# A fused expert-attention-expert block: the last expert queue of phase 2 added on VectorE, values' remainders earlier in attention's first stage, and fewer fillers ahead of it

## The reference

```
x = x + 0.5 * ffn(layernorm(x))       # phase 1: experts "e1"
x = x + attention(layernorm(x))       # 4 heads of 32, delta rule in chunks of 32
x = x + 0.5 * ffn(layernorm(x))       # phase 2: experts "e2"
```

## Time and profile before

| | |
|---|---|
| median of three runs | 917.46 us |
| lowest and highest of them | 914.82 and 926.24 us |
| the profiled execution | 921.84 us, its span 920.0 us |
| PE busy | 845.3 us (92%) |
| DVE busy | 547.2 us (59%) |
| POOL busy | 500.8 us (54%) |
| ACT busy | 392.8 us (43%) |
| mean granted clock of TensorE | 0.953 of full speed |

### The profile page before, as it was taken

The page is one execution under the profiler, slowest core; times in us unless marked ns, Lnnn a source line. Parts: engine busy times, 40 slices in busy tenths (PEclk is TensorE's granted clock), DMA queues, the critical chain, the costliest instruction groups (busy, mean ns, idle before and its releaser), DMA issues. The chain is left out here.

```text
span 920.0 us, 26251 instructions
## 1 busy us (share of the span) xinstructions
PE 845.3 (92%) x10885; PEld 747.1 (81%) x10885; DVE 547.2 (59%) x1645; ACT 392.8 (43%) x850; POOL 500.8 (54%) x631
## 2 busy tenths in 40 slices
PE   8479999999979789999999899998989999999996
PEld 7358999999967566788778776877767899999996
DVE  4745665555557945658485936484573556656662
ACT  4634444444314432266346542562542544444431
POOL 2658889866630721582228623882445444346667
PEclk8569999999989899899999999999998999999998
DMA  9454677444222110012001121111112644445544
GB/s 310 111 117 122 214 232 251 133 137 135 61 85 58 24 33 18 4 24 54 20 5 30 38 75 39 22 35 52 51 47 78 223 154 153 128 128 115 118 67 36
DMA packets 75475, 85.97 MB, mean 93 GB/s; under 512 B 9767, under 2 KB 62163, under 8 KB 74332
## 3 DMA queue, kind: packets, MB, share of 16 engines
q1 hardware_dynamic: 61148, 63.74, 23.3%
q0 software_dynamic: 14208, 20.55, 9.7%
HBM read 46.70 MB, written 34.01 MB: 88 GB/s over the span
## 5 line engine op out<-in xcount | busy, mean ns | idle before, releaser
L1020 DVE TENSOR_TENSOR e_hid<-e_sg,e_pu 128x320 f32<-128x320 f32 x256 | 124.7, 488 | 160.5 <-ACT e_sg L961 153.9
L961 ACT ACTIVATE e_sg<-e_pg 128x320 f32<-128x320 f32 x256 | 111.9, 438 | 208.5 <-PE e_pg L918 208.1
L282 POOL DMA_INDIRECT queue<-wide_rows,slot x64 | 64.9, 1014 | 89.5 <-ACT wide_rows L568 21.1
L1112 POOL TENSOR_TENSOR first_rows<-a_inv,a_nmat 128x135 f32<-128x135 f32 (+20 forms) x116 | 61.2, 527 | 68.7 <-DVE a_nmat L1965 60.2
L916 PE MATMUL e_pg<-e_xlo,e_whi 128*128 128x320 f32 x256 | 96.6, 377 | 0.9 <-DVE e_xlo L983 0.5
L904 PE MATMUL e_po<-e_expert,e_hid 128*128 128x128 f32 x640 | 83.7, 275 | 1.3 <-DVE e_hid L1020 1.3
L904 PE MATMUL e_po<-expert,e_hid 128*128 128x128 f32 x640 | 84.2, 274 | 0.0
L904 PEld LDWEIGHTS e_po<-e_expert,e_hid 128*128 128x128 f32 x640 | 79.9, 191 | 1.8 <-DVE e_hid L1020 1.8
L904 PEld LDWEIGHTS e_po<-expert,e_hid 128*128 128x128 f32 x640 | 80.3, 191 | 0.1
L917 PE MATMUL e_pg<-e_xhi,e_wlo 128*128 128x320 f32 x256 | 79.7, 311 | 0.0
L918 PE MATMUL e_pu<-e_xhi,e_whi 128*128 128x320 f32 x256 | 79.5, 310 | 0.0
(11 more groups left out here) (379 smaller groups left out, 2076.8 us busy)
## 6 DMA issues: line engine op xcount, KB each, us to landing
expert<-wexp_in SPq DMA_DIRECT2D x14, 512.0 KB, 4.4
e_expert<-wexp_in SPq DMA_DIRECT2D x14, 512.0 KB, 4.4
line<-blank SPq DMA_DIRECT2D x3, 1310.0 KB, 7.4
e_xs<-queue SPq DMA_DIRECT2D x12, 327.5 KB, 4.9
e_xs<-line SPq DMA_DIRECT2D x6, 647.5 KB, 6.4
expert<-wexp_in SPq DMA_DIRECT2D x14, 256.0 KB, 2.8
e_expert<-wexp_in SPq DMA_DIRECT2D x14, 256.0 KB, 3.5
queue<-blank SPq DMA_DIRECT2D x2, 1310.0 KB, 9.3
```

The source lines that it names most:

```text
L282: pool.indirect_dma_start(io.queue, bass.IndirectOffsetOnAxis(ap=k.slot[:, j, 1:2], axis=0), k.xn[:, j, :], None, bounds_check=SLOTS - 1, ...
L961: act.activation(sg[n % 2][:], pg[n % 2][:, 0:HALF], ACT.Silu).then_inc(silued, 1)
L1020: dve.tensor_tensor(hid[q % 2][:, f, c * HALF:c * HALF + HALF], sg[n % 2][:], pu[n % 2][:, 0:HALF], ALU.mult).then_inc(hidden, 1)
L1112: link(eng.tensor_tensor(part, bc(inv[:, j:j + 1, own], shape), bc(factor, shape), ALU.mult))
```

## The change

Four edits.

1. **Phase 2's last queue.** Its token numbers and weights are loaded on their own (`ahead`, one transfer on SP's queue in its iteration q = 6) and `index` for it runs in q = 7 on VectorE. After the first eight queues' transfers have landed, POOL gathers the rows of `out` that belong to the last queue's tokens into `rest` (five indirect transfers) and waits for them, then goes on with the tiles of queues 8 to 15. VectorE adds `rest` while it writes out the last queue's products, and POOL sends these with `replace` in place of `add_up`.
2. **The order of the three terms of the scales, in all stages:** the product with `vlo` comes last of three. Of the first half of a group, the first matmul waits for `vhi`, and only the third for `vlo`.
3. **VectorE in attention's first stage:** the second half of `vlo` after step 7 in place of step 10; `low_rows(1)` after step 25, ahead of the last six steps and of `prepare`, in place of after `prepare`. `SPLIT` is 6 in place of 8: VectorE inverts 6 columns, POOL 26.
4. **Fillers:** 40 in place of 56 ahead of attention's first transposes; 10 new ones in the first stage ahead of the scales.

```
+        rest = None if raw else sb("rest", [P, CT, D])
+        ahead = None if raw else sb("ahead", [P, CT, ROW - D])
...
+                if not raw and q + 2 == E:
+                    sp.dma_start(ahead[:], io.queue[SLOTS - CAP:SLOTS, D:ROW].rearrange(
+                        "(s p) d -> p s d", p=P)).then_inc(peeked, 16)
...
-                if half and q // E in BY_TOKEN:
-                    index(q)
+                if half and q // E in BY_TOKEN and (raw or q < LAST):
+                    index(q, rows_of(q)[:, :, D:ROW])
...
+                    if not raw and q == LAST:
+                        dve.wait_ge(foretold, 1)
+                        dve.wait_ge(restored, 16 * CT)
+                    elif not raw:
                         dve.wait_ge(indexed, numbered(q))
...
-                elif q < E:
+                elif q < E or q == LAST:
                     dve.scalar_tensor_tensor(rows[q % NR][:, s, :], down_bank(tile), factor[:, q, s:s + 1],
-                                             rows_of(q)[:, s, ROW:WIDE], ALU.mult, ALU.add).then_inc(rready, 1)
+                                             rows_of(q)[:, s, ROW:WIDE] if q < E else rest[:, s, :],
+                                             ALU.mult, ALU.add).then_inc(rready, 1)
...
+                    if not raw and q + 1 == E and n == REST_AT:
+                        dve.wait_ge(peeked, 16)
+                        index(LAST, ahead[:])
...
-                    put = deliver if raw else replace if q < E else add_up
+                    put = deliver if raw else replace if q < E or q == LAST else add_up
...
                 keep_tiles(0, CT * E)
                 all_stored(pool, 0)
+                pool.wait_ge(foretold, 1)
+                for s in range(CT):
+                    gather(pool, io.out, token[:, LAST, s:s + 1], rest[:, s, :], restored)
+                pool.wait_ge(restored, 16 * CT)
                 keep_tiles(CT * E, CT * NQ)
...
-        SPLIT = 8
+        SPLIT = 6
+        ROWS_IN = 25
...
                     elif first:
-                        pe.wait_ge(silued, UNITS * a + 6 - bank)
+                        pe.wait_ge(vhigh, 2 * a + 2)
+                    if i == TERMS - 1 and not half:
                         pe.wait_ge(vlow, 2 * a + 2)
...
-                        x, w = ((vhi, k.lag_hi), (vlo, k.lag_hi), (vhi, k.lag_lo))[term]
+                        x, w = ((vhi, k.lag_hi), (vhi, k.lag_lo), (vlo, k.lag_hi))[term]
...
+                if not here:
+                    keep_clock(pe, k, pp[:, 0, :], 10)
                 part = filler(6)
...
-            keep_clock(pe, k, pp[:, 0, :], 56)
+            keep_clock(pe, k, pp[:, 0, :], 40)
             turn(0, (0,))
...
                     low_values(a, 0)
-                    invert_first(5, 10)
+                    invert_first(5, 7)
                     low_values(a, 1)
+                    invert_first(7, 10)
                     cross_values(a)
-                    invert_first(10, CHUNK - 1)
+                    invert_first(10, ROWS_IN)
+                    low_rows(g + 2, 0)
+                    low_rows(g + 2, 1)
+                    invert_first(ROWS_IN, CHUNK - 1)
...
                 if ahead:
                     prepare(a)
-                if later:
+                if later and here:
                     low_rows(g + 2, 0)
-                if later:
                     low_rows(g + 2, 1)
```

More of the change, by code:

```diff
@@ L751, in experts @@
         downed, rready, indexed = sem("downed"), sem("rready"), sem("indexed")
+        peeked, foretold, restored = (None if raw else sem(n) for n in ("peeked", "foretold", "restored"))
         stored = [[sem(f"stored{i}") for i in range(NR)], k.delivered] if raw else k.stored
@@ L989, in evacuate @@
                     rows_free(dve, q)
-                    if not raw:
+                    if not raw and q == LAST:
+                        dve.wait_ge(foretold, 1)
+                        dve.wait_ge(restored, 16 * CT)
+                    elif not raw:
                         dve.wait_ge(indexed, numbered(q))
@@ L1000, in evacuate, with index @@
                                       ALU.mult).then_inc(rready, 1)
-            def index(q):
-                row = rows_of(q)
+            def index(q, row):
                 if raw:
-                    dve.tensor_scalar(token[:, q, :], row[:, :, D], float(APART), None, ALU.add).then_inc(indexed, 1)
+                    dve.tensor_scalar(token[:, q, :], row[:, :, 0], float(APART), None, ALU.add).then_inc(indexed, 1)
                 else:
-                    dve.tensor_copy(factor[:, q, :], row[:, :, D + 1 + q // E])
+                    dve.tensor_copy(factor[:, q, :], row[:, :, 1 + q // E])
                     spare = C_TRASH + q % 2 * CT
-                    dve.scalar_tensor_tensor(token[:, q, :], row[:, :, D], float(2 * APART),
-                                             k.const[:, spare:spare + CT], ALU.add, ALU.min).then_inc(indexed, 1)
+                    dve.scalar_tensor_tensor(token[:, q, :], row[:, :, 0], float(2 * APART),
+                                             k.const[:, spare:spare + CT], ALU.add,
+                                             ALU.min).then_inc(foretold if q == LAST else indexed, 1)
             low_weights(0, 0)
@@ L1052, in keep_tiles @@
                     if s == 0:
-                        pool.wait_ge(indexed, numbered(q))
+                        if raw or q < LAST:
+                            pool.wait_ge(indexed, numbered(q))
                         if not raw and q % E >= 2:
@@ L1094, in _ @@
                 all_stored(pool, c)
-        return range(wgot[0].num, (stored[0][NR - 1] if raw else indexed).num + 1)
+        return range(wgot[0].num, (stored[0][NR - 1] if raw else restored).num + 1)
 def behind(eng, sem, value):
@@ L1455, in scales @@
                     elif first:
-                        pe.wait_ge(silued, UNITS * a + 6 - bank)
+                        pe.wait_ge(vhigh, 2 * a + 2)
+                    if i == TERMS - 1 and not half:
                         pe.wait_ge(vlow, 2 * a + 2)
                     if kind == Z_STACKED:
-                        x, w = ((shi, k.lag_hi), (slo, k.lag_hi), (shi, k.lag_lo))[term]
+                        x, w = ((shi, k.lag_hi), (shi, k.lag_lo), (slo, k.lag_hi))[term]
                         start = 0
                     else:
-                        x, w = ((vhi, k.lag_hi), (vlo, k.lag_hi), (vhi, k.lag_lo))[term]
+                        x, w = ((vhi, k.lag_hi), (vhi, k.lag_lo), (vlo, k.lag_hi))[term]
                         start = LAGS - 1 - lag + half * P
```

## The result

| | before | after |
|---|---|---|
| median of 20 runs each, one chip | 920.53 us | 914.49 us |
| profiled execution, span | 921.84, 920.0 us | 913.19, 911.4 us |
| mean granted clock of TensorE | 0.953 | 0.960 |

The ratio is 0.9947 [0.9928, 0.9966], 4.9 us less (3.1 to 6.6); the medians lie 6.0 apart. The forecast was 8.7 less, from a median of three runs that lay 3.1 under that of the twenty. The absolute forecast, 908.8, is 5.7 too low, 3.1 by the median that it started from and 2.6 by the change; the range 902.5 to 916 holds the time.

What follows compares the result with a forecast made beforehand. TensorE is busy nearly throughout, so gains lie only where it waits, runs slowly or has finished. 5.5 us (start and first stage) plus 3.2 (end) make 8.7, from 917.46 to 908.8; range 902.5 to 916.

Steps and rivals of the forecast that it cites:

- The start: Attention's start: 16 fillers fewer make TensorE ready sooner; gain 0.7 us, bounds 0 and 0.71.
- the slower rival: Attention's first stage: clock falls in gaps the 40 fillers leave, stage runs at 1.2 GHz, 923 us; chance 0.05.
- The scales: Attention's first stage: third scales matmul 4.98 us sooner, last one 6.5 sooner, spacing 0.243 at full clock.
- POOL's columns: First stage's inverse: with two more columns POOL takes 24.3 to 28.4 us, done before `prepare`, so costing nothing.
- VectorE's inverse: First stage: VectorE reaches step 25 sooner by 25% less data in eighteen steps, 0 to 4 us, taken as 2.
- four signs: Wrong if clock dips before 300, POOL's columns end after step 31, TensorE waits for shifted copies, or stage 0 lengthens.
- The end: Phase 2's end: last issue 2.3 us sooner, landing 0.9 faster; 3.2 less in all, bounds 2.3 and 3.5.
- The gathers: Phase 2: POOL's five gathers make queue 8's tiles 5.5 us later (9 with longest landing), costing nothing at the end.
- cover of seven queues: Phase 2: 3.15 us idle per queue lets POOL catch up in two or three of the seven queues left.
- The sum: Whole kernel: 5.5 us for start and first stage plus 3.2 at the end, 8.7 less, 908.8.
- The first stage's gain is given back: Attention's stage 0: VectorE's waits and low clock lose 2 to 5 us, giving 911 to 914; chance 0.23.

Runs made afterwards that it cites:

- e9_no10: The changed kernel without the ten new fillers ahead of the scales; ran once, no ratio, last scales matmul 1.53 us later and `solve` 0.72 sooner.
- e7_pool_less: The changed kernel with POOL making only the last two columns of group 0's inverse, part of the computation left out; ran once, no ratio.
- e2_split10: The changed kernel with `SPLIT` 10 in place of 6; median 912.09 us, ratio to the kernel before 0.9912 [0.9879, 0.9945].
- e6_best: The changed kernel with `SPLIT` 10 for 6 and the row remainders after step 27 for 25; median 909.96 us, ratio to before 0.9918 [0.9892, 0.9943].
- e1_split8: The changed kernel with `SPLIT` back at 8 in place of 6; median 913.09 us, ratio to the kernel before 0.9925 [0.9901, 0.9949].
- e3_tail: The kernel before with only the change to phase 2's last queue; median 916.02 us, ratio to before 0.9951 [0.9931, 0.9971].

## Why the prediction was right or wrong

**The start: right.** The first `keys` matmul comes at F+9.44 for F+10.26, 0.82 sooner, forecast 0.7. In all eight profiled kernels with 40 fillers the clock was at its full level before that matmul; the slower rival did not occur. Read in stretches of half a microsecond, the granted clock rose between F+2.7 (e9_no10) and F+6.0 (e7_pool_less), at another point from execution to execution, and the fillers, 5.84 to 7.46 us long, outlasted it each time. That rival's price was also too high: at the lower level a matmul of `keys` takes 0.43 (after, 328.36 to 328.79) for 0.24, 0.19 more and not 0.243.

**The scales: right.** Third matmul 5.16 sooner for 4.98, last one 6.85 for 6.5; spacing 0.24 after the first of that run, as the ten fillers held the clock (e9_no10). SP's copies stalled nothing.

**POOL's columns: right.** 25.8 us, 299.26 to 325.02, inside the forecast's 24.3 to 28.4, and ended 5.1 ahead of `prepare`. That they "cost nothing" was wrong in another way, next.

**VectorE's inverse: the step that failed.** The prediction said that VectorE comes to step 25 sooner "by 25% less data in eighteen steps", "between 0 and 4 us, I take 2". It cost 2 us, 20.20 for 18.22, outside of bounds that excluded a loss without a reason. While both engines substitute, VectorE's step is as long as POOL's, so moving columns to POOL lengthens VectorE's steps, however little data they hold. The trace of before showed it in rows that the prediction did not read; VectorE, and then POOL:

```profile
315.65 0.47 DVE L1112 TENSOR_TENSOR a_u<-a_inv,a_nmat 128x160 f32<-128x160 f32 x1
...
316.69 0.45 DVE L1112 TENSOR_TENSOR a_u<-a_inv,a_nmat 128x152 f32<-128x152 f32 x1
```

```profile
315.50 0.43 POOL L1112 TENSOR_TENSOR first_rows<-a_inv,a_nmat 128x140 f32<-128x140 f32 x1
...
316.55 0.42 POOL L1112 TENSOR_TENSOR first_rows<-a_inv,a_nmat 128x135 f32<-128x135 f32 x1
```

The starts lie 0.15 and 0.14 apart, with 160 elements against 140: a common beat. That POOL's work sets it, e7_pool_less shows. 160 elements took 1.04 a step here, and 126 took 0.64 without POOL (e7_pool_less). From there the chain is as the prediction built it, with another late one: the rows' remainders wait for VectorE and not for ScalarE (F+58.63; ScalarE's first part would have let them start at about F+56.7, for in e2_split10, e6_best and e7_pool_less, where they wait for it, they start 5.9 after the last scales matmul). `keys` starts 1.6 later than forecast, after the idle time of 3.07 the clock is down and costs 1.54 more, and `solve` starts at F+65.38 for F+63.27, released by the end of `keys` and not by `prepare`. e1_split8 takes back this step alone and gets to F+62.47, 0.8 better than the forecast. None of the four signs by which the prediction would have called itself wrong appeared where it failed: it had none for a slower VectorE.

The Trainium skill, "SBUF — State Buffer", section "SBUF: two separate sides", says that VectorE and GpSimd share one pair of ports to SBUF, the on-chip memory of the tiles, as an exclusive lock, and that a VectorE operation with two SBUF inputs contends for it with a GpSimd one that reads SBUF. Both instructions of a step are of that kind, and the trace agrees: 0.56 for 0.28 us on VectorE, and the other way round 1.34 for 0.48 on POOL at 311.71, beside VectorE's product over 128x1024 elements, 1.35 us from 311.35. That it is the ports and not something else that the two share, no run here tells apart.

**The end: right, 0.33 too much.** 2.87 for 3.2: counted from TensorE's end, the last issue comes 1.82 sooner, forecast 2.3, and from there to the end of the span it is 1.05 less, forecast 0.9. Three of the four spacings are 1.27 to 1.32; the one ahead of 906.05 is 1.65, a wait of 0.64 for VectorE's rows.

**The gathers: right that they cost nothing, wrong in their size.** Queue 8's first tile is 10.9 us late, not 5.5, nor the 9 that the prediction gave for the longest landing: 16.02 after the last replacing issue for 5.09 in the earlier trace rows. The two waits for landing lasted 5.48 and 5.32 us from the last issue to the next instruction (818.58 to 824.06, 829.28 to 834.60), where the prediction took medians of 2.5 and 3.0; the 5.09 in the earlier trace rows held such a wait already, and the gathers' came on top. POOL has idle time again at 884.04, in queue 13 and not by queue 11: of the cover of seven queues the change used five.

**The sum.** By the marks the change gives 3.37 at `solve`, the start in it, and 2.87 at the end: 6.2 for 8.7. The medians' 6.0 agrees, and 6.2 lies inside the ratio's 3.1 to 6.6. That the time lies in the range speaks for no mechanism, as the range took in most of the rivals. "The first stage's gain is given back" foresaw the size, but neither the place nor the cause: VectorE does not wait inside the inverse, it runs slower there. What stays open is whether a further microsecond goes in the later stages: the ratios of all kernels with the new first stage lie 0.7 to 2.3 us short of their marks, though e3_tail's lies 1.5 beyond. From the first `solve` to phase 2's first gate matmul the profiled executions take between 375.7 (e3_tail) and 382.0 us (e1_split8), 379.2 before and 378.1 after, so single profiles cannot settle it.

## What to carry to other kernels

Two engines that work beside each other on the same memory may not be independent: compare the starts of their instructions before you move work from one to the other. If they go in step, as here, the share that you take off the one that follows may give it nothing, and what you add to the other slows both. And where a wait is taken away ahead of an engine, cost the next one with the clock in it: the 3.07 us ahead of `keys` were paid for once as idle time and once more, by half (1.54), in slow matmuls.

## What the runs showed of the hardware that was not expected

POOL is hardly slowed by VectorE's short steps, only by its long instruction. With VectorE substituting, POOL's 168-element step takes 1.14 (313.73 to 314.87) and its 160-element step 1.11 (316.02 to 317.13); in stage 0, where VectorE does not substitute, a step over 156 elements takes 1.12 in the changed kernel (376.05 to 377.17):

```profile
376.05 0.46 POOL L1130 TENSOR_TENSOR first_rows<-a_inv,a_nmat 128x156 f32<-128x156 f32 x1
376.58 0.50 POOL L1132 TENSOR_TENSOR a_inv<-a_inv,first_rows 128x156 f32<-128x156 f32 x1
377.17 0.49 POOL L1130 TENSOR_TENSOR first_rows<-a_inv,a_nmat 128x175 f32<-128x175 f32 x1
```

So VectorE pays nearly the whole price of the overlap. And a wait for the last of a row of transfers is not their median: in the changed kernel the two around the gathers lasted 5.48 and 5.32 us from the last issue, where the five replacing transfers ahead of the first wait land in a median of 2.3 (longest 4.6) and the five gathers in a median of 2.7 (longest 4.5).
